# Expert slots of a routed MLP: a transposing transfer in place of TensorE's transposes for every second slot

## The reference

```
t      = rmsnorm(layernorm(x)) * norm_w                  # 2048 x 256
logits = t @ gate_w.T + gate_b                           # 16 experts
vals, idx = top_k(logits, 4); gates = softmax(vals)
h   = t @ w1[e].T + b1[e]                                # 512 wide, for each chosen expert e
act = min(h[::2], 7) * sigmoid(1.702 * min(h[::2], 7)) * (clip(h[1::2], -7, 7) + 1)
y   = act @ w2[e].T + b2[e]                              # 256 wide
x   = x + 0.5 * sum over the 4 experts of gate * y
```

## Time and profile before

| | |
|---|---|
| median of three runs | 1133.45 us |
| the profiled execution, its own time | 1132.82 us |
| its span, first to last instruction | 1131.1 us |
| granted TensorE clock, mean over the span | 0.862 |
| TensorE matmul busy | 739.4 us (65%) |
| VectorE busy | 621.4 us (55%) |
| ScalarE busy | 424.0 us (37%) |
| GpSimd busy | 368.1 us (33%) |
| slots of the first MoE | from about 131 to 373 us of the span |
| slots of the second MoE | from about 852 to 1085 us |

### The profile page before, as it was taken

One profiled execution on the slowest core, in us unless ns is written; L12 is line 12 of the kernel. 1 busy time (PEld: TensorE's weight loads), 2 busy tenths in 40 slices (PEclk: granted clock), 3 DMA queues, 4 the chain that ended last, 5 costly groups with the idle time before them and its releaser, 6 DMA issues. The chain is left out here.

```text
span 1131.1 us, 22067 instructions
## 1 busy us (share of the span) xinstructions
PE 739.4 (65%) x5770; PEld 450.2 (40%) x5770; DVE 621.4 (55%) x1953; ACT 424.0 (37%) x945; POOL 368.1 (33%) x404
## 2 busy tenths in 40 slices
PE   2222068999999305757999999522204999999930
PEld 1121035666666202322353534421202666666620
DVE  5865046566665386336767673371601566665537
ACT  2322045555555202112646455111102555555510
POOL 3766712333333202450000000055672333333320
PEclk9999989999999756775999999755556999999975
DMA  8555322333333453430111110212232333333346
GB/s 303 202 181 180 122 60 74 86 94 96 82 91 97 140 180 96 144 102 2 45 31 45 31 31 3 76 69 89 80 116 75 92 96 95 92 95 94 82 144 228
DMA packets 110387, 114.31 MB, mean 101 GB/s; under 512 B 38836, under 2 KB 96669, under 8 KB 110272
## 3 DMA queue, kind: packets, MB, share of 16 engines
q1 hardware_dynamic: 95008, 73.82, 23.0%
q0 software_dynamic: 15264, 39.10, 9.3%
HBM read 60.89 MB, written 55.56 MB: 103 GB/s over the span
## 5 line engine op out<-in xcount | busy, mean ns | idle before, releaser
L319 POOL DMA_INDIRECT y_rows<-y_m,goal_m x158 | 155.7, 985 | 312.5 <-ACT y_m L482 292.3
L391 PE MATMUL banks<-w1s,rT_m 128*128 x948 | 236.0, 386 | 0.0
L666 DVE TENSOR_SCALAR b_m<-banks 128x256 f32<-128x256 f32 x158 | 67.0, 424 | 212.3 <-ACT p_m L468 126.9
L309 POOL DMA_INDIRECT x_rows<-row_m,row_to_m x128 | 132.5, 1035 | 124.5 <-DVE row_to_m L626 87.0
L1191 DVE CUSTOM_DVE_ANT_0 junk<-banks,maskq 128x128 bf16<-128x128 f32 (+3 forms) x256 | 115.7, 488 | 44.9 <-PE banks L1040 41.7
L461 ACT ACTIVATE rT_m<-banks 128x512 f16<-128x512 f16 x158 | 93.6, 592 | 111.5 <-issue 58.1
L391 PEld LDWEIGHTS banks<-w1s,rT_m 128*128 128x128 f16 x948 | 94.3, 99 | 98.5 <-issue 6.7
L413 PE MATMUL banks<-w2s,hT_m 128*128 x948 | 129.7, 273 | 0.0
L1160 ACT ACTIVATE probs<-banks 128x1024 f32<-128x1024 f32 (+3 forms) x128 | 86.0, 703 | 88.8 <-PE banks L1076 88.7
L373 PE MATMUL banks<-ident,rows_m 128*128 128x128 f16 x632 | 62.7, 223 | 78.0 <-DMA rows_m<-x_rows 40.5
L468 ACT ACTIVATE p_m<-banks 128x256 f32<-128x256 f32 x158 | 60.5, 383 | 110.5 <-PE banks L391 107.7
(11 more groups left out here) (164 smaller groups left out, 1157.9 us busy)
## 6 DMA issues: line engine op xcount, KB each, us to landing
rows_m<-x_rows SPq DMA_DIRECT2D x158, 128.0 KB
arena_m<-y_rows SPq DMA_DIRECT2D x32, 512.0 KB, 5.5
arena_m<-in_w SPq DMA_DIRECT2D x16, 512.0 KB, 6.5
arena_m<-in_w SPq DMA_DIRECT2D x16, 256.0 KB, 7.0
qk_split<-w_raw SPq DMA_DIRECT2D x32, 128.0 KB
x_rows<-pad SPq DMA_DIRECT2D x2, 2040.0 KB, 8.4
q_stack<-qk_split SPq DMA_DIRECT2D x32, 96.0 KB
k_stack<-qk_split SPq DMA_DIRECT2D x32, 96.0 KB
```

What stands on the lines that cost most here:

```text
L309: pool.indirect_dma_start(x_rows[m], bass.IndirectOffsetOnAxis(ap=row_to[:, i, k:k + 1], axis=0), row[:, i % NR, :], None).then_inc(scatte ...
L319: pool.indirect_dma_start(y_rows[m], bass.IndirectOffsetOnAxis(ap=goal[:, c, :], axis=0), y[:, n % NY, :], None, bounds_check=K * T - 1, o ...
L391: mm = pe.matmul(o, rT[:, n % 2, 2 * r + k, :], w1s[:, bass.ds(e, 1), k, w, :], start=False, stop=(k == HC - 1 and w == 1))
L666: dve.tensor_scalar(b[:, n % 2, :], bank[2 + n % 2][:, INNER:], (LIMIT + 1.0) * S, (1.0 - LIMIT) * S, ALU.min, ALU.max).then_inc(ev("b"), 1)
```

## The change

Odd slots are no longer turned by TensorE. Their transfer on SyncE becomes a transposing one (`dma_start_transpose`) that writes the four turned blocks into a ring of its own, `rT_odd`, of 4 slots; `up` of an odd slot reads them there and waits for `loaded` itself. Even slots keep `rows` (now 4 slots), TensorE's transposes and `rT`. The counts of the semaphores `turned` and `rT` run over even slots alone. SyncE waits for slot n-8 to be turned (even n) or for its `up` to be done (odd n), and, as before, for the stored results of slot n-8. On TensorE and ScalarE the order changes: `turn_rows(0)` and `turn_rows(2)` stand before the loop, and the step s, if odd, has `turn_rows(s+3)`; an even step has none.

```diff
-                rows = tmp("rows", [P, NX, 2 * H], f16)
+                rows = tmp("rows", [P, NX // 2, 2 * H], f16)
+                rT_odd = tmp("rT_odd", [P, NX // 2, 4, P], f16)
...
                             if n >= NX:
-                                sp.wait_ge(ev("turned"), n - NX + 1)
+                                if n % 2 == 0:
+                                    sp.wait_ge(ev("turned"), (n - NX) // 2 + 1)
+                                else:
+                                    sp.wait_ge(ev("up"), n - NX + 1)
                                 sp.wait_ge(y_stored[(n - NX) % NY], (n - NX) // NY * 16 + 16)
...
-                            sp.dma_start(rows[:, c, :], x_rows[m].bitcast(f16)[bass.ds(row0, P), 0:2 * H]).then_inc(loaded[c], 16)
+                            src = x_rows[m].bitcast(f16)[bass.ds(row0, P), 0:2 * H]
+                            if n % 2 == 0:
+                                sp.dma_start(rows[:, c // 2, :], src).then_inc(loaded[c], 16)
+                            else:
+                                sp.dma_start_transpose(rT_odd[:, c // 2], src).then_inc(loaded[c], 16)
...
                             pe.wait_ge(loaded[c], 32 * (n // NX) + 32)
-                            if n >= 2:
-                                pe.wait_ge(ev("rT"), n - 1)
+                            if n >= 4:
+                                pe.wait_ge(ev("rT"), n // 2 - 1)
                             for q in range(4):
-                                mm = pe.transpose(bank16[n % 2][:, q * P:(q + 1) * P], rows[:, c, q * P:(q + 1) * P],
-                                                  ident16[:, :])
+                                mm = pe.transpose(bank16[n // 2 % 2][:, q * P:(q + 1) * P],
+                                                  rows[:, c // 2, q * P:(q + 1) * P], ident16[:, :])
...
                         def up(n, e):
-                            pe.wait_ge(ev("rT"), n + 1)
+                            if n % 2 == 0:
+                                pe.wait_ge(ev("rT"), n // 2 + 1)
+                                x_of = rT[:, n // 2 % 2]
+                            else:
+                                pe.wait_ge(loaded[n % NX], 32 * (n // NX) + 32)
+                                x_of = rT_odd[:, n % NX // 2]
...
-                                    mm = pe.matmul(o, rT[:, n % 2, 2 * r + k, :], w1s[:, bass.ds(e, 1), k, w, :], start=False,
+                                    mm = pe.matmul(o, x_of[:, 2 * r + k, :], w1s[:, bass.ds(e, 1), k, w, :], start=False,
...
                         turn_rows(0)
-                        turn_rows(1)
+                        turn_rows(2)
                         for s in range(SLOTS + 2):
                             if s < SLOTS:
                                 up(s, held[s])
-                            if s + 2 < SLOTS:
-                                turn_rows(s + 2)
+                            if s % 2 == 1 and s + 3 < SLOTS:
+                                turn_rows(s + 3)
...
                         def rows_out(n):
-                            act.wait_ge(ev("turned"), n + 1)
-                            if n >= 2:
-                                act.wait_ge(ev("up"), n - 1)
+                            act.wait_ge(ev("turned"), n // 2 + 1)
+                            if n >= 4:
+                                act.wait_ge(ev("up"), n - 3)
...
                         rows_out(0)
-                        rows_out(1)
+                        rows_out(2)
...
-                            if s + 2 < SLOTS:
-                                rows_out(s + 2)
+                            if s % 2 == 1 and s + 3 < SLOTS:
+                                rows_out(s + 3)
```

More of the change, by code:

```diff
@@ L457, in rows_out @@
                         def rows_out(n):
-                            act.wait_ge(ev("turned"), n + 1)
-                            if n >= 2:
-                                act.wait_ge(ev("up"), n - 1)
-                            act.activation(rT[:, n % 2], bank16[n % 2][:, 0:512].rearrange("p (q n) -> p q n", q=4),
+                            act.wait_ge(ev("turned"), n // 2 + 1)
+                            if n >= 4:
+                                act.wait_ge(ev("up"), n - 3)
+                            act.activation(rT[:, n // 2 % 2], bank16[n // 2 % 2][:, 0:512].rearrange("p (q n) -> p q n", q=4),
                                            ACT.Copy).then_inc(ev("rT"), 1)
```

## The result

The changed kernel took 1208.15 us (median of four, 1202.12 to 1212.7) against 1134.29 us of the kernel before in the same comparison: a ratio of 1.0642, 95% interval 1.0583 to 1.0702. It was forecast slower, at 1151.5 us within 1136 to 1205: the sign was right, the loss is four times the one forecast, and the median lies just above the range. The profiled execution took 1212.70 us with a span of 1211.0 us.

A forecast was written before the change was run, and what follows sets the result against it. The prediction took TensorE, at 2.72 us per slot with loads only narrowly ahead, to bound the kernel. Its terms, -17.2 + 31.0 + 5.0 = +18.8 us on 1132.82, gave 1151.6, say 1151.5 us, range 1136 to 1205.

The forecast's parts named there:

- What bounds the kernel: Slot stage: TensorE, busy nearly throughout, sets the pace at 2.72 us per slot; loads are prefetched with a small margin.
- Part 1: TensorE in odd slots: 78 groups of four transposes removed, 0.22 us each, 17.2 us saved; shorter activation cover costs nothing.
- Part 2: Even slots' turn_rows, one step earlier, stalls TensorE on goal loads: 72 x 0.43 = 31.0 us lost (21.6 to 41.0).
- the window from `down(n-8)`: TensorE's time from `up` in the step of down(n-8) to turn_rows(n): 8.00 us before, 7.56 us after the change.
- half the lack: TensorE comes 0.60 to 1.13 us too early; two stalls share each window, so each is 0.30 to 0.57, taken as 0.43.
- the prediction's own halving: Two stalls lie in each 7.56 us window, so each need be only half of what TensorE comes too early.
- Part 3: Start of each MoE: up(0) now needs slots 0 and 2; +2.4 us in the second, 0 to 2.8 in the first, together 5.
- Part 4: SyncE's transposing transfer for odd slots: near a plain load, costed at nothing; bounds nothing or 1 us more (+16 us).
- the slack of 0.55: On SyncE: a slot costs 2.17 of 2.72 us, so an odd slot may take 0.55 us more before loads are late.
- The slow transfer: Transposing transfer holds the queue over 2.7 us, delaying even slots' rows: 1195 us at 3.9, 1238 at 5.1; chance 0.16.
- The estimate of 5.2 us: Transposing transfer of an odd slot: four blocks in line at 1309 ns per 128x128 block of 16-bit numbers.
- The rival of no stall: At turn_rows(n) even rows come in time, 7.41 us, under 7.56: faster, 1120.6 us; chance 0.10.

The follow-up runs named there:

- experiment 4: Changed kernel with turn_rows(n) back in step n-2 for even n and plain transfers for odd slots (left unturned): 1124.79 us, ratio 0.9893 to the kernel before.
- experiment 2: Kernel before with only turn_rows of even slots one step earlier, all turned by TensorE, all transfers plain: 1207.28 us, ratio 1.0624; run again, 1.0569.
- experiment 5: Changed kernel with goal a ring of 16 instead of 8: 1090.47 us against 1079.44 for the kernel before, ratio 1.0108; run again, 1.0139.
- experiment 6: Kernel before with turn_rows of even slots one step earlier, transfers plain, goal a ring of 16: 1083.06 us against 1079.44, ratio 1.0031.
- experiment 3: Changed kernel with plain transfers in place of transposing ones for odd slots, which stay unturned: 1202.19 us, ratio 1.0576 to the kernel before.
- experiment 1: Changed kernel with turn_rows(n) back in step n-2 for even n, transposing transfers kept: 1150.91 us, ratio 1.0109 to the kernel before.
- experiment 7: Changed kernel with turn_rows(n) back in step n-2 for even n and goal a ring of 16: 1084.3 us against 1079.44 for the kernel before, ratio 1.0042.

## Why the prediction was right and wrong

**What bounds the kernel**: right. TensorE's pace and the small margin of the loads were the two things that mattered.

**Part 1, the removed transposes, 17.2 us**: right within what can be told, 13.6 us in experiment 4. That the shorter cover of the activation chain costs nothing held there too: TensorE is busy 183 of 185 us.

**Part 2, the moved `turn_rows`, 31.0 us**: this is the step that failed, in its size. The mechanism is as written: the place, the `goal` transfer as what is waited for, the window from `down(n-8)`, the sign. Experiment 2 shows it alone at 62 to 69 us, experiments 5 and 6 show that it hangs on the stored results. What was mis-sized is "each need be only half the lack: 0.30 to 0.57 us, and I take 0.43". Per pair of slots, in the stage of 35 pairs of the second MoE:
- the waits for `goal` themselves are 19.9 / 35 = 0.57 us, at the upper end. The arrival was taken from one slot, 8.16 to 8.69 us after `up` ends. Over the 35 even slots from 10 to 78 of the second MoE of the kernel before the mean is 8.93 (scatter to row issue 3.63, not 3.25; `goal` issue to landing 1.83), and none is under 8.08. The data of a mean were in the trace; I read one slot. By the prediction's own halving the mean gives (8.93 - 7.56) / 2 = 0.69 us, 49 us in place of 31.0, and 1170 us: a third of the miss.
- after a wait there is a second gap before `turn_h`, 8.6 us in all, 0.25 per pair. It was not in the sum.
- the rest, 0.39 per pair, was not in the sum either. It is of two parts. The first is the end of a matmul, which the gaps shown leave out. In a full stream the next instruction starts before it: 0.23 us behind the start of four transposes (949.99 and 950.22 in the earlier trace rows), though they last 0.39. The gaps shown count from the end, so each costs 0.16 us more than it shows. Slot 11 has it at the full clock:

```profile
943.60 1.46 PE L404 MATMUL banks<-w1s,rT_odd_m 128*128 x6
946.29 0.40 PE L381 MATMUL banks<-ident,rows_m 128*128 128x128 f16 x4 [1.23 <-DMA goal_m<-x_rows]
947.05 0.38 PE L413 MATMUL banks<-ident,hs_m 128*128 128x128 f16 x4 [0.37 <-issue]
948.25 0.59 PE L404 MATMUL banks<-w1s,rT_m 128*128 x2
```

From 943.60 to 948.25 are 4.65 us; such a slot takes 2.72 without gaps, the gaps shown are 1.60, and 0.33 us are not shown, 0.16 for each of the two gaps. In the 63 of the 70 slots that had the full clock throughout this comes to 7.1 us. The second part is the clock: the 7 slots that touch the 13.5 us of the lower level have 7.4 us above their gaps. Together 14.5 us, 0.41 per pair, of which the kernel before has 0.02 to 0.03 too. In experiment 2 the lower clock was granted for 3.4 us only; there 0.2 per pair remains, 5.2 us of such ends and 2.0 us of the clock.

The three are the pair's 6.46 us (2 x 3.23) less 5.25 (2 x 2.73 less 0.22). A stall of 1 us cost about 2. By the terms: 0.57 + 0.25 + 0.39 = 1.21 us per pair, where 0.43 was forecast; times 72 it is 87 us, less 17.2, plus 8.8 for the start and the first slots (3.25 + 2.7 + 2.8), is 79, against 79.9 between the spans of the two profiled executions and 74 between the medians. The parts are read from the traces; no run here kept the waits and took the lower clock or the second gap away.

**Part 3, the start, 5 us**: right in kind and too small, 8.8 us. `up(0)` of the second MoE starts 16.3 us after the first `goal` issue instead of 13.6, 2.7 later (forecast 2.4); in the first MoE slot 8 is 3.25 us late (forecast 0 to 2.8). The 2.8 us more that slots 0 to 7 of the second MoE take were not in it. Most of them are one stall of part 2: the transposes of slot 10, behind `up(7)`, wait for `goal` until 932.14, 1.52 us, and 0.46 us follow before `turn_h`.

**Part 4, the transposing transfer**: half right. Its landing and its hold on the queue are nothing, 1.0 us of transfer, and `up` of an odd slot never shows a wait for its load. Its issue is 1.22 us, 0.88 over a plain one: within the bounds (nothing to 1 us more), and over the slack of 0.55 that I gave it, where I had taken nothing. In the changed kernel that is mostly hidden behind the waits (experiment 3, 0.5 to 0.7 of a per cent). At the old distance it is what remains, 26 us (experiments 1 and 4), of which the ring of 16 takes perhaps 8 (experiment 7), and it is why half of the slots can't be given to transposing transfers from SyncE for a gain. A single slot's slack of 0.55 was the wrong measure: a pair takes TensorE 5.22 us in a full stream and now costs SyncE 5.25.

**The rivals.** The slow transfer, to which I gave 0.16 and which would have given 1195 to 1238 us, has nearly the measured time and is wrong: the queue is free after 2.2 us, and with plain transfers the time is 1202 us all the same (experiment 3). Its sign, a `goal` landing 3 us or more behind its issue, is there in 3 of 34 even slots, as in the kernel before. A result close to a rival's price doesn't show the rival. The rule of the Trainium skill (Advanced Engine Details and Errata, X-Bar Transpose), that transposing transfers are as fast as plain ones, holds for the transfer (1.0 us for 128 KB, against 0.9) and not for the issue (1.22 us against 0.34). The estimate of 5.2 us from the figure of the Trainium skill (VectorE: DVE Perf Modes, The three transpose paths) is refuted by the same row: the four blocks took 1.0 us. The rival of no stall did not occur.

## What to carry to other kernels

Before a consumer is moved up by a step, measure how long its data have been there over all its instances, not one, and follow the load back to what frees its buffer: here a small ring of 4-byte addresses, and not the large ring of rows, held the prefetch, and doubling it showed no cost (experiment 6 is 3.6 us over the kernel before, the later start included). Price a stall of a saturated TensorE at more than its length, since the stream has to run out and start again, and a second gap and a lower clock can follow (here 1 us cost about 2). A transposing transfer took the DMA engines no longer than a plain one, but its issuer 0.88 us more, so count the issuing engine's time per step before giving it work that TensorE did.

## What the runs showed of the hardware that was not expected

- The issue of a transposing transfer of 128 x 512 16-bit numbers holds SyncE for 1.22 us (1.207 at the least over the 78 of experiment 7), a plain one of the same bytes for 0.34; the transfer takes 1.0 us at up to 258 GB/s.
- After a wait of 2.21 us TensorE's granted clock fell to the lower level and the next six matmuls of 512 columns took 2.46 us instead of 1.46.
- After each wait in `turn_rows` TensorE shows a further 0.35 to 0.6 us before `turn_h`, though what `turn_h` needs is there: 17 times of 17 in the stage from 934 to 1160 us.
- The same program took 5% less on one chip than on the others (1079 against 1134 to 1138 us). The deeper ring of experiment 5 has a trace on both: spans of 1085.0 and 1151.5 us, but its slots 8 to 78 differ by 1 us in the first MoE and 3 in the second, so some 62 of the 66.5 us lie outside of them.
